# Last row of windows: a new order on three engines, two tiles of xn on VectorE, fillers on TensorE

## What is computed

```
x = x + outlook(gn(x))        # per token softmax over a 3x3 neighbourhood, 6 heads, weighted sum of v
x = x + windows(gn(x))        # shifted 7x7 windows: softmax(q k^T + bias + mask) v, 12 heads
outlook(x) = sum_k softmax(x Wa + ba)[k] * shift_k(x Wv + bv) @ Wp + bp
windows(x) = roll(unwindow(attention(window(roll(x)))) @ Wproj + bproj)
gn(x)      = (x - mean_group) / sqrt(var_group + 1e-5)
```

## Time and profile before

| | |
|---|---|
| median of three runs | 3562.01 us (3558.45 to 3566.17) |
| the profiled execution, time and span | 3563.42 us, 3561.6 us |
| TensorE busy | 3295.9 us, 93% of the span |
| VectorE busy | 2763.4 us, 78% |
| GpSimd busy | 2300.7 us, 65% |
| ScalarE busy | 1840.1 us, 52% |
| mean granted TensorE clock | 0.959 |

### The profile page before, as it was taken

How to read it: one execution, slowest core, us unless ns; L and a number is a source line. 1 busy time by engine, 2 the same in 40 slices (tenths; PEclk the granted TensorE clock), 3 DMA queues, 4 the chain that set the end, 5 groups by cost and what they waited for, 6 DMA issues and landing times.

```text
span 3561.6 us, 105414 instructions
## 1 busy us (share of the span) xinstructions
PE 3295.9 (93%) x39908; PEld 1971.8 (55%) x39908; DVE 2763.4 (78%) x4561; ACT 1840.1 (52%) x3506; POOL 2300.7 (65%) x1889
## 2 busy tenths in 40 slices
PE   6999989899898998989989899899999999999998
PEld 3356654566445664456634666346663466634666
DVE  4968869678796886968879677786878878687786
ACT  3445644466445654455543565435654456543565
POOL 2857747677486774767647676576765767466674
PEclk7999989999999999999999999999999999899998
DMA  4732327322362323713256122561225513165132
GB/s 103 137 87 70 87 67 142 81 64 83 86 136 67 86 79 82 145 44 87 79 104 132 48 76 76 108 132 56 80 61 121 119 55 87 58 132 108 51 87 64
DMA packets 204335, 317.44 MB, mean 89 GB/s; under 512 B 16922, under 2 KB 176154, under 8 KB 203802
## 3 DMA queue, kind: packets, MB, share of 16 engines
q0 software_dynamic: 31936, 148.66, 21.4%
q1 hardware_dynamic: 171866, 161.61, 15.9%
HBM read 45.97 MB, written 38.54 MB: 24 GB/s over the span
## 4 chain that ended last, share of the span: by engine, by line
PE 35%; issue 25%; POOL 24%; DVE 6%; DMA 5%; ACT 4%; POOLq 1%; DVEq 0%; ACTq 0%; SPq 0%
POOL sp__70 L1787 9%; POOL sp__70 L1780 7%; DMA prod<-prod 5%; PE P L488 4%; DVE prod L1423 3%; POOL xw L1766 2%; POOL xr L1773 2%; PE P L733 2%; PE P L720 2%; PE P L654 2%; PE P L493 2%; PE P L699 1%; PE P L656 1%; PE P L756 1%; PE P L506 1%
## 5 line engine op out<-in xcount | busy, mean ns | idle before, releaser
L1787 POOL TENSOR_TENSOR sp__70<-sp__70,rc 128x588 f32<-128x588 f32 x512 | 600.6, 1174 | 495.0 <-DVE rc L1552 483.1
L1423 DVE TENSOR_TENSOR prod<-P,vpad 128x896 f32<-128x896 f32 (+1 forms) x768 | 791.2, 1051 | 132.1 <-PE P L488 117.0
L1780 POOL TENSOR_TENSOR sp__70<-sp__70,mx 128x588 f32<-128x588 f32 x512 | 600.9, 1174 | 192.5 <-DVE mx L1542 191.9
L1118 ACT ACTIVATE sp__70<-sp__70 128x588 f32<-128x588 f32 x512 | 356.7, 698 | 597.5 <-POOL sp__70 L1780 597.3
L1549 DVE TENSOR_REDUCE sm<-sp__70 128x12 f32<-128x588 f32 x512 | 389.9, 761 | 282.2 <-ACT sp__70 L1118 281.8
L1535 DVE TENSOR_TENSOR sp__70<-P,relb 128x588 f32<-128x588 f32 x512 | 389.3, 760 | 153.5 <-PE P L720 145.0
L488 PE MATMUL P<-at,sel 108*128 108x448 bf16 x1512 | 425.2, 360 | 62.4 <-DVE prod L1423 32.2
L1700 POOL DMA_DIRECT2D prod<-prod x216 | 202.7, 941 | 359.0 <-DVE prod L1423 355.2
L1542 DVE TENSOR_REDUCE mx<-sp__70 128x12 f32<-128x588 f32 x512 | 389.7, 761 | 9.3
L733 PE MATMUL P<-ident,sp__70 113*98 113x113 f32 x3072 | 356.9, 267 | 26.9 <-DVE sp__70 L1535 16.6
L733 PEld LDWEIGHTS P<-ident,sp__70 113*98 113x98 f32 x3072 | 324.8, 132 | 96.6 <-issue 54.4
(11 more groups left out here) (257 smaller groups left out, 7177.2 us busy)
## 6 DMA issues: line engine op xcount, KB each, us to landing
prod<-prod POOLq DMA_DIRECT2D x216, 672.0 KB, 5.5
vbd<-vs SPq DMA_DIRECT2D x512, 147.0 KB
xin<-in_x SPq DMA_DIRECT2D x126, 336.0 KB, 5.2
out<-ot SPq DMA_DIRECT2D x184, 168.0 KB, 4.2
out<-ot SPq DMA_DIRECT2D x80, 84.0 KB
wn<-in_L_conv_qkv_weight SPq DMA_DIRECT2D x2, 432.0 KB, 6.7
wno<-in_L_conv_proj_weight SPq DMA_DIRECT2D x2, 144.0 KB, 7.0
self<-in_sel SPq DMA_DIRECT2D x3, 91.1 KB
```

Of the source, the lines that this page charges most:

```text
L1118: go(sp_[:, b, :], sp_[:, b, :], ACT.Exp).then_inc(p_exp, 1)
L1423: tt(by_row(dst), by_row(P[:, b:b + len(op), 0:CT]), val, ALU.mult).then_inc(prod_ok, 1)
L1780: tt(per_head(sp_[:, b, :]), per_head(sp_[:, b, :]), spread(mx[:, b, :]), ALU.subtract).then_inc(t_sub, 1)
L1787: tt(per_head(sp_[:, b, :]), per_head(sp_[:, b, :]), spread(rc[:, b, :]), ALU.mult).then_inc(p_norm, 1)
```

## The change

Only the last row and the end of row 6 change. PE: `turn_out(w - 2, 2)` and `turn_out(w - 2, 3)` follow attend(0); `begin_out` of row 6 leaves its place behind group_variances and follows turn_probs(2), directly ahead of `end_out`; `turn_logits` moves ahead of turn_probs(3); fillers stand behind group_variances (4), behind attend(2) (4), between logits and turn_logits (2) and behind turn_logits (4). ACT: all three `keep_next` first, the exponents of step 3 ahead of `keep_probs` of step 2, `exps` ahead of two `keep_out`, and only one tile of xn. DVE: two `stat_x` go to the end of row 6, the others and `aggregate` are spread behind the chain of step 2, and two tiles of xn are made here. POOL's list stays as it is.

```diff
@@ between_last (PE)
-                        turn_out(w - 2, 2, R2)
                     elif p == 2:
+                        pe.wait_ge(ot_kept, ONE + NT * (R - 1))
+                        begin_out(w - 1, (R1, R0), R2, freed=(g_std, ONE + 2 * i + 3))
                         end_out(w - 1, (R1, R0), R2)
@@ after_last (PE)
                     if p == 0:
-                        pe.wait_ge(ot_kept, ONE + NT * (R - 2) + 3)
-                        turn_out(w - 2, 3, R2)
+                        turn_out(w - 2, 2, R2)
+                        pe.wait_ge(ot_kept, ONE + NT * (R - 2) + 2)
+                        turn_out(w - 2, 3, R1)
                         group_means(2 * i + 2, R0)
                     elif p == 1:
                         group_variances(2 * i + 2, R0)
-                        pe.wait_ge(ot_kept, ONE + NT * (R - 1))
-                        begin_out(w - 1, (R1, R0), R2, freed=(g_std, ONE + 2 * i + 3))
+                        stay_warm(4, R1)
                     elif p == 2:
+                        stay_warm(4, 0)
                         pe.wait_ge(fin_ok, ONE + T * R)
                         logits(Gn, NEXT_BANK)
-                    else:
+                        stay_warm(2, 0)
                         turn_logits(Gn, NEXT_BANK)
+                        stay_warm(4, 0)
@@ last_row (ACT)
                     keep_next(w, 0, R2)
-                    keep_probs(w, 0, 0)
                     keep_next(w, 1, R0)
                     keep_next(w, 2, R1)
+                    exp_step(w, 1, 0)
+                    keep_probs(w, 0, 0)
...
-                    keep_probs(w, 2, 0)
-                    keep_probs(w, 2, 1)
                     act.wait_ge(g_ready, ONE + 2 * i + 3)
                     act.wait_ge(y_mm, ONE + STEPS * (NW * i + w))
-                    normalize(Gn, 0)
+                    normalize(Gn, 0, (0,))
                     exp_step(w, 3, 0)
                     exp_step(w, 3, 1)
+                    keep_probs(w, 2, 0)
+                    keep_probs(w, 2, 1)
                     keep_logits(Gn, NEXT_BANK)
@@ last_row (DVE)
-                    stat_x(i + 1, w - 2, range(T))
+                    stat_x(i + 1, w - 2, (2,))
+                    stat_x(i + 1, w - 1, (0,))
                     prob_sum(w, 1, 0)
-                    stat_x(i + 1, w - 1, range(T))
+                    stat_x(i + 1, w - 1, (1,))
+                    prob_sum(w, 1, 1)
+                    score_bias(w, 2, 0)
+                    score_bias(w, 2, 1)
+                    score_max(w, 2, 0)
+                    stat_x(i + 1, w - 1, (2,))
+                    score_max(w, 2, 1)
+                    keep_y(w, 0)
                     aggregate(2 * i + 2, x_stat, T * CHUNKS * (i + 2))
-                    prob_sum(w, 1, 1)
-                    ahead(w, 0)
-
+
+                    prob_sum(w, 2, 0)
                     deviate(2 * i + 2, R0)
-                    prob_sum(w, 2, 0)
...
                     coefficients(2 * i + 2)
+                    dve.wait_ge(g_ready, ONE + 2 * i + 3)
+                    dve.wait_ge(y_mm, ONE + STEPS * (NW * i + w))
+                    for j in (1, 2):
+                        ts(xn[:, j, :].rearrange("p (r n) -> p r n", n=W), xa[:, j, 0:ROWS, 0:W],
+                           ga[:, j:j + 1], gb[:, j:j + 1], ALU.mult, ALU.add).then_inc(xn_ok, 1)
```

More of the change, by code:

```diff
@@ L962, in keep_x, with normalize @@
                    P[:, bank, 0:CT].rearrange("p (r n) -> p r n", n=W), ACT.Copy).then_inc(x_kept, 1)
-            def normalize(G, c):
+            def normalize(G, c, tiles=range(T)):
                 act.wait_ge(l_mm, ONE + G)
                 act.wait_ge(v_mm, ONE + T * G)
-                for j in range(T):
+                for j in tiles:
                     go(xn[:, j, :].rearrange("p (r n) -> p r n", n=W), xa[:, j, c * ROWS:(c + 1) * ROWS, 0:W],
@@ L1192, in window_row @@
                         w2, p2 = pair_after(w, p, 2)
-                        exp_step(w2, p2, 0)
+                        if (w2, p2) != (NW - 1, 1):
+                            exp_step(w2, p2, 0)
                 def last_row():
@@ L1204, in last_row @@
                     keep_out(w - 2, 2, R2)
+                    keep_out(w - 2, 3, R1)
                     exp_step(w, 2, 0)
-                    keep_out(w - 2, 3, R2)
                     keep_probs(w, 1, 0)
@@ L1213, in last_row @@
                     load_table(4 * i + 5, ACT.Exp)
+                    act.wait_ge(g_ready, ONE + 2 * i + 3)
+                    act.wait_ge(y_mm, ONE + STEPS * (NW * i + w))
+                    normalize(Gn, 0, (0,))
+                    exp_step(w, 3, 0)
+                    exp_step(w, 3, 1)
                     keep_probs(w, 2, 0)
                     keep_probs(w, 2, 1)
-                    act.wait_ge(g_ready, ONE + 2 * i + 3)
-                    act.wait_ge(y_mm, ONE + STEPS * (NW * i + w))
-                    normalize(Gn, 0)
-                    exp_step(w, 3, 0)
-                    exp_step(w, 3, 1)
                     keep_logits(Gn, NEXT_BANK)
@@ L1225, in last_row @@
                     keep_probs(w, 3, 1)
+                    exps(Gn, NEXT_BANK)
                     keep_out(w - 1, 0, R1)
                     keep_out(w - 1, 1, R2)
-                    exps(Gn, NEXT_BANK)
                     keep_out(w - 1, 2, R1)
@@ L1596, in window_row @@
                             wrap_out(w - 1)
+                            if w == NW - 2:
+                                stat_x(i + 1, w - 1, (0, 1))
                         elif w >= 2 and p == 0:
```

## The result

The changed kernel takes 3599.94 us (median of four runs, 3584.99 to 3611.88), the kernel before 3564.09 us beside it: a ratio of 1.0101, 95% interval 1.0069 to 1.0132. A second set of four, beside nineteen runs of before, gave 3599.91 us and 1.0111 (1.0076 to 1.0145). So it is slower, by about 36 us, where the forecast said 25: the sign is right, the size too small, and 3600 stood at the upper end of the range.

The account below looks back on a forecast made before the run. PE was taken to bound the kernel, with POOL's softmax steps behind. Per row 2.0 for aggregate, 0.9 behind group_variances and 0.2 behind logits make 3.1 us; eight rows give 25: 3562 + 25 = 3587 us, range 3566 to 3600.

Parts of the forecast that it names:

- Its sum for pair 6: The last row of a pass, read in pair 6 as representative: 3.1 us longer, removed idle time included.
- Aggregate comes later, 2.0 us: DVE's new order ends aggregate later, so group_means and everything behind it on PE start 2.0 us later.
- Behind group_variances, 0.9 us: PE from group_variances to logits: fillers and low-clock turn_probs(2) bring logits to 2.9 us late, 0.9 beyond aggregate's 2.0.
- Behind logits, 0.2 us: PE from logits to values_wide: 7.1 us instead of 6.86, with turn_logits and fillers ahead of turn_probs(3), 0.2 more.
- POOL's own wait would shrink: POOL ahead of normalize_step(3): its 9.29 us idle should shrink, as step 3's exponents start about 3 us earlier.
- Eight times pair 6: All eight last rows were taken to lose pair 6's 3.1 us each, giving 25 us.
- nothing changes: PE from the start of group_means to the end of group_variances: stays 11.53 us at low clock.
- fell late: Clock full for group_means and turn_probs(1), low afterwards: 0.6 us a row, 3567 us; chance 0.11.
- the first rival: TensorE's clock stays full through the row: values_wide 3.0 us sooner, 24 us less in eight rows, 3538 us; chance 0.10.
- the third rival: Clock returns over 6 us behind group_variances, begin_out takes 4.08 us: row 4.8 us longer, 3600 us; chance 0.12.

Follow-up runs that it names:

- second trace: The changed kernel, unaltered, run and profiled once more beside the kernel before: 3599.91 us, ratio 1.0111.
- The gap filled: The changed kernel with 18 more fillers on PE directly ahead of group_means: 3568.19 us, 1.0008 of the kernel before.
- reordered version: The changed kernel without its fillers, with stat_x(w-1, 2), aggregate, deviate, keep_probs(1) and prob_sum(3) moved earlier: 3544.55 us, 0.9942 of the kernel before.
- early aggregate: The changed kernel with DVE's stat_x(w-1, 2) and aggregate directly behind stat_x(w-1, 1): 3569.72 us, 1.0015 of the kernel before.
- 7 fillers: The reordered version with three fillers ahead of turn_probs(1) and four ahead of scores(3): 3534.95 us, 0.9928 of the kernel before.

## Why the prediction was right or wrong

Its sum for pair 6 was 3.1 us; that row is 3.66 longer (45.00 to 48.66). Over all eight rows it is 4.15.

- **Aggregate comes later, 2.0 us.** Right: group_means went from 6.79 to 8.83 us, released by aggregate, with 3.87 us idle (about 4 forecast) and the clock falling in it. That the clock would stay low up to group_variances was right as well (11.63 us against 11.53 from start to start).
- **Behind group_variances, 0.9 us.** Mis-sized; it was 1.5 (9.74 against 8.24). Four fillers took 1.66 (1.6 forecast), turn_probs(2) 2.39 and not 2.0, begin_out 2.59 and not 2.38, since the clock returned somewhat later than the 3.6 us taken from the earlier trace rows; the other terms were within 0.1.
- **Behind logits, 0.2 us.** It was 0.0 (6.87 against 6.86). Turn_probs(3) did not wait, as forecast: POOL was done at 2682.92, 1.44 us ahead of it (about 1.5 forecast), so the four fillers there covered nothing, as said. That POOL's own wait would shrink was wrong; finish ahead of prob_sum(3) on DVE was overlooked. On PE it cost nothing here.
- **Eight times pair 6.** This is the step that failed by most, and with it the term that was put at nothing: from the start of group_means to the end of group_variances "nothing changes". That holds for pair 6 and the four other rows that were at half clock before (11.6 us there, 11.6 to 11.8 after). But the rows before were not alike: in three of them the clock was up for group_means and this stretch took 8.8, 8.9 and 10.0 us. The earlier trace rows showed one of them beside pair 6; the two better ones took 43.3 us as a whole. The changed kernel has the gap in every row, so all of them go to 49. By means over the eight rows, aggregate cost 1.8 us (2.0 forecast), the stretch that was to stay the same 1.0 (nothing forecast) and all behind it 1.4 (1.1 forecast): 48.96 - 44.81 = 4.15 a row, 33 us, against 3.1 and 25. The better rows were read for the clock and not for what the change takes away from them. The remaining few us up to the measured 36 can't be placed: the second trace has 29 us in its rows.
- **The rivals.** The clock neither stayed full nor fell late. The gap filled shows what the first rival would have needed: fillers in the wait itself. There the clock stayed at 1.00 through group_means. By the Trainium skill, "TensorE: Matmul & The Clock Gate", section "What's actually happening", activity releases the throttle; the fillers ahead of group_means, which kept the clock up, agree with that, those of the change, behind group_variances, made the low stretch neither reliably shorter nor longer. The return was not late enough for the third rival either: 4.3 to 5.6 us behind group_variances.

What the prediction did not see is why the 2.0 us cost what they cost: not the wait alone, but PE idle in it. With the wait filled, group_means came as late and the row was 4.7 us shorter (3.0 where both versions are without the change's own fillers). What is lost behind group_variances is the fillers: from its end to the row's end it takes 28.4 us with them and 25.5 without, where it took 27.0 before.

## What to carry to other kernels

Where an engine must wait in front of several short steps, look at what its clock does in that wait before moving its release: the delay counted 2 us and the half-clock stretch behind it kept it, while fillers inside the gap won back 3.0 to 4.7 us a row and fillers behind it cost 1.4 to 3.05. When rows of a kernel fall into better and worse ones, multiply the mean of what the change does to each kind, not the worst. And a gain in one stage is only a gain when the stages behind it are read again, and in more than one trace, since the clock's falls there differ from run to run.

## What the runs showed of the hardware

The clock fell with little idle time: in the reordered version's row of pair 6 the longest waits of PE ahead of the fall were 0.63 us, ahead of scores(2), and 0.56 us, between fourteen one-column matmuls and turn_probs(1), and the granted clock went to 0.5 at 8.4 us (8.1 to 9.4 in the eight rows). The stretches of pair 6, from 3.6 and from 8.6 us:

```profile
2632.00:2636.00 4.00, 3.41 (x71) 3.02 (x64) 3.92 (x11) 0.86 (x2) 2.01 (x2) 1.00 0.58 169
2637.00:2640.00 3.00, 2.25 (x91) 1.85 (x94) 2.90 (x8) 2.75 (x5) 1.77 (x3) 0.50 0.00 0
```

Seven fillers in the waits on either side of turn_probs(1) moved the fall to 12.6 us or later in all eight rows.

A short DVE operation took seven times as long while POOL worked. DVE's squaring of 128x3 in deviate, in the reordered version:

```profile
2637.48 1.18 DVE L1293 TENSOR_TENSOR gdev<-gdev 128x3 f32<-128x3 f32 x1
```

with POOL busy from 2636.34 to 2638.64, and in the changed kernel, where POOL was idle from 2661.11 to 2666.93:

```profile
2662.48 0.16 DVE L1297 TENSOR_TENSOR gdev<-gdev 128x3 f32<-128x3 f32 x1
```

It ended with POOL's operation: this one at 2638.66, and in the traces of before, early aggregate, reordered and 7 fillers every DVE operation on 128x3 that took over 0.4 us ended 0.01 to 0.02 us behind one of POOL's. Not every short operation is held up: `gdev<-mv,P`, which reads one input from PSUM, took 0.15 us with POOL busy in the reordered version. The two go together in these rows; it was not tested by itself.
